# The second cross-attention of a Perceiver kernel moved into the block before it, its bias constants summed on GpSimd

## The reference

```python
# first layer's MLP: weights are +1/-1 from booleans; 1024 -> 2048 -> 2048 -> 512
h = concatenate([x, -x], -1); h = relu(s0 * (h @ w(k0))) * 2; h = relu(s1 * (h @ w(k1))) * 2; h = s2 * (h @ w(k2))
# second layer's cross-attention (one head over all 512 columns)
Q = input_1 @ Wq + bq;  K = input_2 @ Wk + bk;  V = input_2 @ Wv + bv
S = clip(Q K^T * scale, -100, 100);  out = softmax(S) V
```

## Time and profile before

| | us |
|---|---|
| median of 3 runs (lowest, highest) | 1212.85 (1212.16, 1214.77) |
| the profiled execution, its own time | 1213.19 |
| its span in the trace | 1211.4 |
| TensorE busy | 1101.9 (91% of the span) |
| VectorE busy | 578.3 |
| ScalarE busy | 377.1 |
| GpSimd busy | 193.5 |

### The profile page before, as it was taken

One profiled execution on the slowest core, in us unless ns is written; L12 is line 12 of the kernel. 1 busy time (PEld: TensorE's weight loads), 2 busy tenths in 40 slices (PEclk: granted clock), 3 DMA queues, 4 the chain that ended last, 5 costly groups with the idle time before them and its releaser, 6 DMA issues. The chain is left out here.

```text
span 1211.4 us, 17827 instructions
## 1 busy us (share of the span) xinstructions
PE 1101.9 (91%) x6507; PEld 678.1 (56%) x6528; DVE 578.3 (48%) x995; ACT 377.1 (31%) x1012; POOL 193.5 (16%) x187
## 2 busy tenths in 40 slices
PE   7999999999899999999998999956998999994986
PEld 4544457887344444444443655456696868773542
DVE  2233145886732322411112544266848475668766
ACT  1211135666311001210001222244424233246863
POOL 0011001333222310000000112025122121300004
PEclk9999999999999999999998999978999999997999
DMA  9964802001011100000007777740000000007001
GB/s 345 387 233 165 312 1 70 2 1 36 26 35 35 41 2 1 1 0 0 0 1 258 269 278 277 278 173 1 1 1 0 0 0 0 0 0 286 1 1 70
DMA packets 55128, 108.61 MB, mean 90 GB/s; under 512 B 4144, under 2 KB 4528, under 8 KB 55088
## 3 DMA queue, kind: packets, MB, share of 16 engines
q1 hardware_dynamic: 55088, 108.09, 25.1%
HBM read 105.98 MB, written 2.10 MB: 89 GB/s over the span
## 5 line engine op out<-in xcount | busy, mean ns | idle before, releaser
L1705 ACT ACTIVATE f_act<-bank,f_sgn 128x512 f32<-128x512 f32 x64 | 44.0, 687 | 267.8 <-PE bank L1660 262.3
L1660 PE MATMUL bank<-f_a_hi,f_w 128*128 128x512 f16 x512 | 115.7, 379 | 0.0
L1660 PE MATMUL bank<-f_a_lo,f_w 128*128 128x512 f16 x512 | 115.7, 379 | 0.0
L1734 DVE CAST f_b_hi<-f_act 128x512 f32 x32 | 25.5, 796 | 165.6 <-ACT f_act L1705 165.6
L1660 PEld LDWEIGHTS bank<-f_a_lo,f_w 128*128 x512 | 50.1, 98 | 60.4
L1660 PEld LDWEIGHTS bank<-f_a_hi,f_w 128*128 x512 | 50.1, 98 | 60.2
L653 POOL TENSOR_TENSOR x_mv<-x_mv,eps 128x2 f32<-128x2 f32 x9 | 1.7, 192 | 439.2 <-DVE x_mv L534 439.2
L1510 DVE TENSOR_TENSOR s_e<-s_pair,s_tables 128x512 f32<-128x512 f32 x64 | 41.4, 687 | 42.0 <-POOL s_kT L1570 24.8
L373 PE MATMUL bank<-x_cT,x_qT 128*64 128x512 f32 x256 | 60.3, 616 | 0.0
L398 PE MATMUL bank<-x_cN,x_eT 128*64 128x512 f32 x256 | 56.9, 596 | 0.0
L1392 ACT ACTIVATE s_e<-bank,s_nmax 128x64 f32<-128x64 f32 x128 | 38.0, 336 | 50.3 <-DVE s_nmax L1456 50.3
(11 more groups left out here) (315 smaller groups left out, 2263.8 us busy)
## 6 DMA issues: line engine op xcount, KB each, us to landing
x_cT<-in_ctx_cols_dram SPq DMA_DIRECT2D x32, 1024.0 KB, 7.6
x_cN<-in_ctx_rows_dram SPq DMA_DIRECT2D x32, 1024.0 KB, 9.5
f_upper_bits<-in_f_w_dram SPq DMA_DIRECT2D x20, 256.0 KB, 2.7
s_wv_raw<-in_s_wv_dram SPq DMA_DIRECT2D x3, 1024.0 KB, 10.7
f_raw<-in_f_wd_dram SPq DMA_DIRECT2D x1, 2816.0 KB, 17.6
x_qw<-in_x_qw_dram SPq DMA_DIRECT2D x8, 256.0 KB, 4.4
x_kw<-in_x_kw_dram SPq DMA_DIRECT2D x8, 256.0 KB, 4.9
x_vw<-in_x_vw_dram SPq DMA_DIRECT2D x2, 1024.0 KB, 14.6
```

The lines of the kernel that those rows point to most:

```text
L1660: mm = pe.matmul(h_bank[s][:, :], weights(2 * i + s, k), part[:, k, cols], start=(n == 0 and k == 0), stop=(n == 1 and k == k_chunks - 1))
L1705: act.activation(act32[s][:, :], h_bank[s][:, :], ACT.Relu, scale=sgn[:, layer % 2:layer % 2 + 1]).then_inc(h_read, 1)
L1734: dve.tensor_copy(hi[:, 2 * i + s, :], act32[s][:, :]).then_inc(hhi_ok, 1)
```

## The change

The second cross-attention becomes part of the first block. `sign_mlp` returns three pairs of semaphore and value. SyncE waits for them before the weights of x1 (`h_done` at 48, the end of layer 0 of the second half), before its context columns (`h_done` at 64) and before its context rows (`y_read` at 10, the end of the MLP). The first `phases.close()` and `end_phase()` go. The value weights load right behind the first bias. M goes to banks 0, 1, 4 and 5, and TensorE waits for `y_read` before its third product. `bk_rep` goes; GpSimd, ahead of its first layernorm step, sums qw rows times bk and kw rows times bq over the four chunks, and bq times bk, and TensorE sums over the partitions by products with ones: one of 128x512, five of one column. Buffers of x1 move: weights, constants and `aT` to the right side of the on-chip memory, `cT` and `cN` to the front of the left side.

```diff
@@ -161,7 +161,7 @@
...
-                    biases=None, clip=None, ahead=(), x=None, identity=None, following=None):
+                    biases=None, clip=None, ahead=(), x=None, identity=None, following=None, context=None, outputs=None, freed=None):
...
@@ -179,26 +179,34 @@
...
+        far = lambda n, s, d=F32, stack=st: stack.enter_context(nc.sbuf_tensor(f"{tag}_{n}", s, d, side="right"))
         if proj is None:
-            v_lo = sb("v_lo", [P, KC, D], F32R)
+            with ExitStack() as early:
+
+                vw_sb = far("vw", [P, KC, D], stack=early)
+            v_lo = far("v_lo", [P, KC, D], F32R)
             v_hi = sb("v_hi", [P, KC, D], F32R)
-        bias_sb = sb("bias", [P, D])
+        else:
+            vw_sb = sb("vw", [P, KC, D])
+        bias_sb = (sb if proj is not None else far)("bias", [P, D])
...
+            bq_sb = far("bq", [P, KC])
+            bk_sb = far("bk", [P, KC])
+            ones = far("ones", [P, P])
+            q_mix = far("q_mix", [P, D])
+            k_mix = far("k_mix", [P, D])
+            b_mix = far("b_mix", [P, KC])
+            b_sum = far("b_sum", [P, 3])
+            term = far("term", [P, D])
+            dots = sb("dots", [P, D])
...
-            dots = bk_rep[:, :, :].rearrange("p k n -> p (k n)")
...
-            aT_hi = slot("aT_hi", [P, KC, P], F32R)
-            aT_lo = slot("aT_lo", [P, KC, P], F32R)
+            aT_hi, aT_lo = outputs
...
-        cT = slot("cT", [P, 2, KC, CTX])
-        cN = slot("cN", [P, 2, MC, D])
+        cT, cN = context if context is not None else (slot("cT", [P, 2, KC, CTX]), slot("cN", [P, 2, MC, D]))
...
+        M_BANK = [4, 5, 6, 7] if biases is None else [0, 1, 4, 5]
...
@@ -269,6 +277,8 @@
...
         @block.sync
         def _(sp):
+            if freed is not None:
+                sp.wait_ge(*freed["weights"])
             for k in range(KC):
                 for dst, src in ((qw_sb, qw), (kw_sb, kw)):
                     sp.dma_start(dst[:, k, :], src[k * P:(k + 1) * P, :]).then_inc(qk_in[k], 16)
...
             sp.dma_start(bias_sb[:, :], out_bias.partition_broadcast(P)).then_inc(small_in, 16)
+            if context is not None:
+                sp.dma_start(vw_sb[:, :, :], vw.rearrange("(c p) n -> p c n", p=P)).then_inc(v_in, 16)
             if proj is not None:
                 sp.dma_start(mask_i[:, :], mask).then_inc(small_in, 16)
             else:
                 sp.dma_start(bq_sb[:, :], biases[0]).then_inc(small_in, 16)
-                sp.dma_start(bk_sb[:, :, :], biases[1].rearrange("p (c o) -> p c o", o=1)).then_inc(small_in, 16)
+                sp.dma_start(bk_sb[:, :], biases[1]).then_inc(small_in, 16)
+            if freed is not None:
+                sp.wait_ge(*freed["context"])
             for s in range(2):
                 for b in range(2):
                     sp.dma_start(cT[s][:, b, :, :], cols_v[s, :, b, :, :]).then_inc(ct_in[s], 16)
             if x is not None:
                 sp.dma_start(xres[:, 2:TILES, :], tiles[:, 2:TILES, :]).then_inc(rest_x_in, 16)
+            if freed is not None:
+                sp.wait_ge(*freed["rest"])
             for s in range(2):
                 for b in range(2):
                     sp.dma_start(cN[s][:, b, :, :], rows_v[s, :, b, :, :]).then_inc(c_in[s], 16)
-            sp.dma_start(vw_sb[:, :, :], vw.rearrange("(c p) n -> p c n", p=P)).then_inc(v_in, 16)
+            if context is None:
+                sp.dma_start(vw_sb[:, :, :], vw.rearrange("(c p) n -> p c n", p=P)).then_inc(v_in, 16)
             if proj is not None:
                 sp.dma_start(proj_sb[:, :, :], proj.rearrange("(c p) n -> p c n", p=P)).then_inc(v_in, 16)
...
@@ -337,7 +354,9 @@
             for k in range(KC):
                 pe.wait_ge(qk_in[k], 32)
                 for c in range(KC):
-                    mm = pe.matmul(bank[4 + c][:, :], qw_sb[:, k, c * P:(c + 1) * P], kw_sb[:, k, :], start=(k == 0), stop=(k == KC - 1))
+                    if freed is not None and k == 0 and c == 2:
+                        pe.wait_ge(*freed["rest"])
+                    mm = pe.matmul(bank[M_BANK[c]][:, :], qw_sb[:, k, c * P:(c + 1) * P], kw_sb[:, k, :], start=(k == 0), stop=(k == KC - 1))
...
@@ -345,15 +364,11 @@
             transpose_x(0)
             if biases is not None:
 
-                pe.wait_ge(prep, 1)
-                for k in range(KC):
-                    mm = pe.matmul(bank[0][:, :], bk_rep[:, k, :], qw_sb[:, k, :], start=(k == 0), stop=(k == KC - 1))
-                for k in range(KC):
-                    mm = pe.matmul(bank[1][:, KC:KC + 1], bk_rep[:, k, :], bq_sb[:, k:k + 1], start=(k == 0), stop=(k == KC - 1))
+                pe.wait_ge(prep, 2)
+                pe.matmul(bank[6][:, :], ones[:, :], q_mix[:, :], start=True, stop=True)
                 for c in range(KC):
-                    for k in range(KC):
-                        mm = pe.matmul(bank[1][:, c:c + 1], kw_sb[:, k, c * P:(c + 1) * P], bq_sb[:, k:k + 1],
-                                       start=(k == 0), stop=(k == KC - 1), skip_group_check=True)
+                    pe.matmul(bank[7][:, c:c + 1], k_mix[:, c * P:(c + 1) * P], ones[:, 0:1], start=True, stop=True, skip_group_check=True)
+                mm = pe.matmul(bank[7][:, KC:KC + 1], ones[:, :], b_sum[:, 2:3], start=True, stop=True, skip_group_check=True)
                 mm.then_inc(rows_done, 1)
...
@@ -468,7 +483,7 @@
...
-                act.copy(m_hi[:, c, :], bank[4 + c][:, :]).then_inc(m_hi_ok, 1)
+                act.copy(m_hi[:, c, :], bank[M_BANK[c]][:, :]).then_inc(m_hi_ok, 1)
...
@@ -571,17 +586,15 @@
...
-            else:
-                dve.tensor_copy(bk_rep[:, :, :], bk_sb[:, :, 0:1].to_broadcast([P, KC, P])).then_inc(prep, 1)
             for c in range(KC):
                 dve.wait_ge(m_hi_ok, c + 1)
-                dve.tensor_tensor(m_lo[:, c, :], bank[4 + c][:, :], m_hi[:, c, :].bitcast(F32), ALU.subtract).then_inc(m_lo_ok, 1)
+                dve.tensor_tensor(m_lo[:, c, :], bank[M_BANK[c]][:, :], m_hi[:, c, :].bitcast(F32), ALU.subtract).then_inc(m_lo_ok, 1)
             split_x(0)
             if proj is None:
                 dve.wait_ge(rows_done, 1)
-                dve.tensor_scalar(w_row[:, :], bank[0][:, :], scale, None, ALU.mult)
-                dve.tensor_scalar(u_col[:, :], bank[1][:, 0:KC], scale, None, ALU.mult)
-                dve.tensor_scalar(row0[:, :], bank[1][:, KC:KC + 1], scale, None, ALU.mult).then_inc(dve_prep, 1)
+                dve.tensor_scalar(w_row[:, :], bank[6][:, :], scale, None, ALU.mult)
+                dve.tensor_scalar(u_col[:, :], bank[7][:, 0:KC], scale, None, ALU.mult)
+                dve.tensor_scalar(row0[:, :], bank[7][:, KC:KC + 1], scale, None, ALU.mult).then_inc(dve_prep, 1)
                 dve.wait_ge(dve_prep, 1)
...
@@ -654,6 +667,26 @@
...
+            if biases is not None:
+
+                pool.wait_ge(small_in, 16 * n_small)
+                pool.memset(ones[:, :], 1.0).then_inc(prep, 1)
+                for n, (mix, weights, by) in enumerate(((q_mix, qw_sb, bk_sb), (k_mix, kw_sb, bq_sb))):
+                    for k in range(KC):
+                        pool.wait_ge(qk_in[k], 32)
+                        if k:
+                            pool.wait_ge(mix_ok, 7 * n + 2 * k - 1)
+                        part = term if k else mix
+                        pool.tensor_scalar(part[:, :], weights[:, k, :], by[:, k:k + 1], None, ALU.mult).then_inc(mix_ok, 1)
+                        if k:
+                            pool.wait_ge(mix_ok, 7 * n + 2 * k)
+                            pool.tensor_tensor(mix[:, :], mix[:, :], term[:, :], ALU.add).then_inc(mix_ok, 1)
+                    pool.wait_ge(mix_ok, 7 * n + 7)
+                pool.tensor_tensor(b_mix[:, :], bq_sb[:, :], bk_sb[:, :], ALU.mult).then_inc(mix_ok, 1)
+                pool.wait_ge(mix_ok, 15)
+                pool.tensor_tensor(b_sum[:, 0:2], b_mix[:, 0:2], b_mix[:, 2:4], ALU.add).then_inc(mix_ok, 1)
+                pool.wait_ge(mix_ok, 16)
+                pool.tensor_tensor(b_sum[:, 2:3], b_sum[:, 0:1], b_sum[:, 1:2], ALU.add).then_inc(prep, 1)
...
@@ -1764,6 +1797,7 @@
...
+        return {"weights": (h_done, 3 * HC), "context": (h_done, 4 * HC), "rest": (y_read, TILES + 2)}
...
@@ -2181,20 +2215,25 @@
...
-        sign_mlp(core, block, "f0", w0, upper, *sign_inputs, io["f0_w1"], io["f0_w2"], sgn, out_scale, bits_read)
-        phases.close()
+        freed = sign_mlp(core, block, "f0", w0, upper, *sign_inputs, io["f0_w1"], io["f0_w2"], sgn, out_scale, bits_read)
         sign_stack.close()
-        core.end_phase()
         held = ExitStack()
         on_chip = {n: core.sbuf(held, f"s1_w{n}_ahead", [P, KC, 2 * D]) for n in "kq"}
         with ExitStack() as st:
-            qw, kw = (core.sbuf(st, f"x1_{n}", [P, KC, D]) for n in ("qw", "kw"))
-            m_hi, m_lo = (core.sbuf(st, f"x1_{n}", [P, KC, D], F32R) for n in ("m_hi", "m_lo"))
```

(32 more changed lines are left out.)

## The result

The changed kernel takes 1201.16 us, median of 4 runs (1200.11 to 1202.74), against 1212.51 for the kernel before: ratio 0.9901, 95% interval 0.9887 to 0.9914. Two later comparisons gave 0.9907 (0.9889 to 0.9924) and 0.9907 (0.9891 to 0.9922). So it is faster by 11.4 us in the medians, by 12.0 us by the ratio. The forecast was 1197.7, 15.15 us faster; applied to the median of 1212.85 that I worked from, the ratio gives 1200.8, the very end of my range, and the median as it was measured lies 0.4 us outside. The sign was right and the gain was put 3 to 4 us too large. The profiled execution took 1200.49 (span 1198.7, 12.7 us shorter than before).

A forecast was written before the change was run, and what follows sets the result against it. TensorE, busy 91% of the span, was taken as the bound. Gains of 8.39 + 5.84 + 1.51 less 0.59 give 15.15 us off the profiled 1213.19: 1198.04, or 1197.7 on the median, range 1196.2 to 1200.8.

The forecast's parts named there:

- M and the gap: Boundary of the two blocks: TensorE's 5.75 us gap goes and M's 32 instructions take 13.73 us for 16.37; gain 8.39 us.
- Bias constants: On TensorE behind M: fewer bias products, so the query projection starts 2.85 us after the transposes begin; gain 5.84 us.
- projection: Query projection up to the first scores: 5.92 us at full clock instead of 7.43; gain 1.51 us.
- Work beside the path: GpSimd's sums during the MLP, 19 to 29 us, done by about 545, slowing VectorE only within its idle time; no cost.
- The clear: End of the second cross-attention: one merged semaphore clear costs the sum of both, 594 and 304 ns; 0.59 us lost.
- The failed step: Everything after the first scores: later turns and stages are the same instructions, shifted; no gain or loss entered for them.
- The prediction's own sign of being wrong: Among the signs listed as showing the prediction wrong: a turn of the attention gets longer than before.
- the first: Rival: clock falls anyway in the projection, or VectorE's row work overruns its cover; price 1.5 us, 1199.2, chance 0.14.
- VectorE's cover of 1.2 us: VectorE's row work ends 8.35 us after the bias products; TensorE wants it after 9.5 us, leaving 1.2 us.
- The slow rival: Loads come only behind the MLP, so GpSimd's sums delay the normalized tiles; 6.0 us slower, 1218.9, chance 0.02.
- The third rival: Only the bias part pays: a gap of some 2 us at the boundary drops the clock; 1202.3, chance 0.06.

The follow-up runs named there:

- merge_only: The changed kernel with the old way to make the bias constants (40 one-column instructions and 8 of 128x512), block still joined; ratio 0.9975 to the kernel before.
- late_bias: The changed kernel with GpSimd's output-bias additions waiting until VectorE has normalized the next turn's tiles; median 1188.2 us, ratio 0.9792 to the kernel before.
- bias_only: The kernel before with only the new bias constants, two separate blocks and loads at the old time; ratio 1.0126 to the kernel before.
- late_weights: The changed kernel with SyncE's first wait, for the weights, moved from chunk 48 to the MLP's end; ratio 1.0106 to the kernel before.
- shift: The changed kernel with two needless float32 products ahead of M, 1.72 us more work; median 1199.95 us, ratio 0.9904 to the kernel before.
- warm_last: The changed kernel with 16 needless products in TensorE's wait in the second cross-attention's last turn; median 1198.55 us, ratio 0.9876 to the kernel before.
- warm_again: Second run of the changed kernel with 16 needless products in the last turn's wait; median 1199.72 us, ratio 0.9881 to the kernel before.

## Why the prediction was right in direction and too large

- **M and the gap** (8.39 us): right. Measured 8.97, of which 0.41 is the MLP's earlier end in this execution: 8.56. (The last 0.17 is that the group of M starts before the modelled end of the MLP's.) No wait for `y_read`, no fall of the clock.
- **Bias constants** (5.84) and **projection** (1.51): right to the hundredth against the kernel before. Made one after the other the two parts are worth something else: with the old bias products in the joined block the clock falls earlier, so the bias part adds 8.9 us there instead of 7.35, and the joined block alone brings 1.6 us less than its 8.39 (merge_only).
- **Work beside the path**: right. Sums done at 539.5 (said 545), 23.5 us long (said 19 to 29), VectorE stretched within its idle time. By the Trainium skill's page GPSIMD Engine Reference, section "Key points", the subtraction with two inputs should suffer; it did (0.69 to 0.99 us), without cost in time. The cast and x̂, which read one such tensor, were stretched more (0.43 to 1.39 us, 544 to 1478 ns); whether they run in the two-port mode that the page also names, no trace here shows. The same sharing costs 13 us elsewhere, in the waits for x̂ of five turns and the low clock behind them (late_bias). I had both x̂ rows in hand, 1.00 and 2.92 us, and used them only to clear the change.
- **The clear** (0.59 lost): right, 0.57 in the clear and 0.16 more in the drain, which I had left out.
- **The failed step** is the sentence "All later turns and stages are the same instructions, shifted", from which the sum took nothing for them. They are the same instructions, but TensorE's clock is not the same under them: 1.85 us in the turns (1.6 of them one low stretch), 0.1 in the rotary attention and 0.9 in the last stage came back. I had taken the clock where the change touches it from rows, and had taken it everywhere else as fixed. The prediction's own sign of being wrong, a turn that gets longer than before, came: the last turn took 26.4 us for 24.7.
- **How far the cause is known.** Three traces of the changed kernel have the stretch in the turns, two of the kernel before have none. But the joined block is neither needed for it (bias_only) nor enough (merge_only, late_weights, shift), and the low clock of one kernel differs between executions, in place (third or fourth turn, 72 us) and in size (6.1 and 9.0 us in the last stage). The stretches lie at waits that both kernels have. Why one wait is followed by a fall and the next is not stays open.
- **The sum of it.** 15.15 us were forecast and 12.7 measured between the profiled executions: 3.0 us of losses that were not in the sum (1.85, 0.1, 0.9 and the drain's 0.16) less 0.6 more gain than forecast at M. The medians differ by about 1 us more (a gain of 11.35 to 12.0): the profiled executions of the changed kernel, 1200.49, 1199.69 and 1201.52, lie below the medians. That part was not traced.
- **The rivals**: the first did not come. The projection ran at clock 1.00, and VectorE's cover of 1.2 us held. That its price, 1.5 us, is near the 1.6 us lost in the turns is luck, and so is that the range, which was widened upwards for this rival, nearly reaches the measured time. The slow rival's mechanism is shown twice; its condition was not met, by more than 100 us as said, and its price was 13 us, not 6: its sum had 19 us for GpSimd's work instead of 22.7 and nothing for the low clock behind the wait. The third rival did not come.

## What to carry to other kernels

Joining two phases pays by the idle gap, the weights' flight and the low clock behind it, and the three together could be read from the trace to 0.2 us; but keep back a part of what the clock gives, since low stretches of 1.6 us came in turns that had none before, and two executions of one kernel differed by 2.6 us in their sums of low clock (warm_last, warm_again). Work moved onto an idle engine must be looked at in that engine's own order: here the sums stand ahead of a layernorm step, and loads that came late would have turned 12 us gained into 13 lost. When a row shows two engines slowing each other, ask where in the kernel TensorE waits for the slowed one; moving 1.3 us additions a few us later was worth as much as the whole change.

## What the runs showed of the hardware that I had not expected

The granted clock falls among one-column products even with no idle time ahead of them: in merge_only TensorE works without a gap from the MLP on, M and the bias products of 128x512 at 1.00, the one-column products run from 658.73 to 664.2, and the clock is 0.99 until 662 and 0.50 from 662 on. With 10 of them in place of 40 (the changed kernel) it stays at 1.00. The clear of the joined set of semaphores, 875 ns, costs nearly the sum of the two, 594 and 304. And two executions of one kernel that agree within 0.1 us up to 1083 us (warm_last and warm_again: 1083.02 and 1082.97 at the last stage's first product) lose 6.1 and 9.0 us to the low clock in the last stage, so one execution does not fix that term.
